# Half of the down columns of an FP4 feed-forward as products of bare values, and a first gated block in another order

## What is computed

```python
def _dequant_fp4(packed_i32, scales_f16, group_size):      # group_size 128
    shifts = jnp.arange(8, dtype=jnp.uint32) * 4
    nib = w[:, :, None] >> shifts & jnp.uint32(15)
    vals = _FP4_LUT[nib.astype(jnp.int32)].reshape(out_f, in_p * 8)
    s_full = jnp.repeat(scales_f16.astype(jnp.float32).T, group_size, axis=1)
    return vals * s_full
gate_up = jnp.einsum('bsh,oh->bso', x, w_gu)
gate, up = (gate_up[..., :I], gate_up[..., I:])            # I = 1408
h = jax.nn.silu(gate) * up
y = jnp.einsum('bsi,hi->bsh', h, w_down)                   # [512, 1408]
return y / jnp.sqrt(jnp.mean(y * y, axis=-1, keepdims=True) + EPS)
```

## Time and profile before

| | us |
|---|---|
| three runs | 937.88, 939.9, 940.07 (median 939.9) |
| profiled execution | 938.71 |
| its span | 936.7, mean granted TensorE clock 0.991 |
| stage 1 | 0 to 223 |
| first feed-forward | 225 to 527 |
| gated part | 527 to 738 |
| routed feed-forward and tail | 738 to 937 |

### The profile page before, as it was taken

One profiled execution on the slowest core, in us unless ns is written; L12 is line 12 of the kernel. 1 busy time (PEld: TensorE's weight loads), 2 busy tenths in 40 slices (PEclk: granted clock), 3 DMA queues, 4 the chain that ended last, 5 costly groups with the idle time before them and its releaser, 6 DMA issues.

```text
span 936.7 us, 13839 instructions
## 1 busy us (share of the span) xinstructions
PE 905.9 (97%) x4976; PEld 720.6 (77%) x4976; DVE 649.7 (69%) x1252; ACT 398.8 (43%) x680; POOL 299.3 (32%) x270
## 2 busy tenths in 40 slices
PE   9999999998999999999999988999999999999994
PEld 7777877886788888888777766786867878888883
DVE  6756753578987798798679676757689886644413
ACT  6443122222443634644573656455554364322221
POOL 1000100002877434434333322131226332734343
PEclk9999999999999999999999998999999999999997
DMA  8633101203210000000010200010201444142311
GB/s 284 182 94 120 47 23 46 79 14 84 52 34 1 1 1 0 1 1 1 7 38 1 101 1 1 1 45 1 90 1 24 158 157 124 51 131 75 128 68 45
DMA packets 43973, 54.20 MB, mean 58 GB/s; under 512 B 6113, under 2 KB 25858, under 8 KB 43906
## 3 DMA queue, kind: packets, MB, share of 16 engines
q1 hardware_dynamic: 42082, 49.11, 16.4%
q0 software_dynamic: 1824, 4.22, 1.4%
HBM read 42.78 MB, written 10.52 MB: 57 GB/s over the span
## 4 chain that ended last, share of the span: by engine, by line
PE 63%; DVE 6%; issue 3%; ACT 2%; POOL 1%; DVEq 0%; ACTq 0%; POOLq 0%
PE ps L41 14%; PE ps L43 14%; PE ps L42 14%; PE ps L2309 8%; PE ps L2310 8%; DVE acc L1697 2%; PE ps L2341 1%; PE ps L2415 1%; PE ps L2401 1%; PE ps L2427 1%; PE ps L2408 0%; DVE junk L1894 0%; DVE state L1795 0%; PE ps L2552 0%; PE ps L2498 0%
## 5 line engine op out<-in xcount | busy, mean ns | idle before, releaser
L1697 DVE SCALAR_TENSOR_TENSOR acc<-ps,gu_scale,acc 128x512 f32<-128x512 f32 x264 | 197.3, 748 | 47.7 <-ACT acc L1370 28.0
L2309 PE MATMUL ps<-xt_hi,gu_val 128*128 128x512 f32 x352 | 140.6, 399 | 3.6 <-PEq L71 1.9
L2310 PE MATMUL ps<-xt_lo,gu_val 128*128 128x512 f32 x352 | 137.3, 390 | 0.0
L1370 ACT ACTIVATE acc<-ps,gu_scale 128x512 f32<-128x512 f32 x88 | 60.7, 689 | 94.2 <-PE ps L2310 94.1
L2213 POOL TENSOR_TENSOR fsg<-fsg,acc 128x512 f32<-128x512 f32 x44 | 59.3, 1348 | 108.5 <-DVE acc L1697 104.4
L2309 PEld LDWEIGHTS ps<-xt_hi,gu_val 128*128 128x128 f32 x352 | 66.0, 188 | 28.6 <-DVE acc L1697 10.9
L666 POOL TENSOR_TENSOR a_rstd<-a_var,minus_half 128x1 f32<-128x1 f32 x14 | 9.0, 644 | 208.2 <-DVE a_var L553 208.2
L2310 PEld LDWEIGHTS ps<-xt_lo,gu_val 128*128 128x128 f32 x352 | 66.1, 188 | 12.1
L2218 POOL TENSOR_TENSOR fh_lo<-fsg,fh_hi 128x512 fp32r<-128x512 f32 x44 | 57.7, 1311 | 42.7 <-ACT fh_hi L1382 42.7
L41 PE MATMUL ps<-dn_hi,fh_hi 128*128 128x512 f32 x176 | 69.3, 394 | 0.0
L42 PE MATMUL ps<-dn_hi,fh_lo 128*128 128x512 f32 x176 | 68.7, 390 | 0.0
(11 more groups left out here) (297 smaller groups left out, 2166.7 us busy)
## 6 DMA issues: line engine op xcount, KB each, us to landing
mw_raw<-in_w SPq DMA_DIRECT2D x16, 512.0 KB, 3.6
a_nib<-in_gate_up_packed SPq DMA_DIRECT2D x88, 64.0 KB, 2.4
x<-x SPq DMA_DIRECT2D x16, 256.0 KB, 2.9
mw_raw<-x SPq DMA_DIRECT2D x8, 512.0 KB, 4.3
out<-mw_raw SPq DMA_DIRECT2D x8, 512.0 KB, 3.0
xt_raw<-in_xT SPq DMA_DIRECT2D x3, 1024.0 KB, 5.3
x<-in_x SPq DMA_DIRECT2D x3, 1024.0 KB, 5.9
...
```

Source lines behind the costliest of these rows:

```text
L1370: act.activation(acc[part][u // 2 % 2][:, :], ps[:, FG, :], ACT.Copy, scale=gu_scale[:, part * IT + j, 0:1]).then_inc(s_g0, 1)
L1697: dve.scalar_tensor_tensor(out=a[:, :], in0=ps[:, FG + c, :], scalar=gu_scale[:, part * IT + j, c:c + 1], in1=a[:, :], op0=ALU.mult, op1=A ...
L2309: pe.matmul(ps[:, FG + c, :], gu_val[:, o, c, :], xt_hi[b % 2][:, c, :], start=True, stop=False)
L2310: pe.matmul(ps[:, FG + c, :], gu_val[:, o, c, :], xt_lo[b % 2][:, c, :], start=False, stop=True).then_inc(s_gu, 1)
```

## The change

1. **Down columns 256 to 511** (CB = 256, two chunks of 128, NA = 2) become `down_bare(k)`: four matmuls of 512 columns with the unscaled FP4 values as weights and the high and low part of h as moving data. They give the transposed sum of one unit, [column, token], in banks FY + 2 and FY + 3. ScalarE takes both out with the column's scale (`take_bare`), GpSimd adds them up in SBUF (`add_bare`). After a block, eight transposes bring the sums back to rows (`transpose_bare`: unit 3 of the next block, unit 4 for the last, and in the gated block for the last), and ScalarE copies them (`take_chunk`).
2. **Down columns 0 to 255** stay as three products, now of 256 columns, two token tiles in a bank; at each block's start a matmul with zeros clears each of the two banks. `take` becomes `take_pair`. The scale rows are half as long.
3. **Order in the stage**: the first four `down_weights` stand ahead of the first `product`; ScalarE copies bare values in units 0 to 3 of block 0; ROWS 4 to 5, in the last block 6 to 7; the squares move behind the transposes; FRONT_SUMS 4 to 5.
4. **First gated block**: `project_qk(1)` stands whole in tile 3, `transpose_qk(1)` and half of `gate_x(0, 3)` ahead of the last `transpose_o`; sigmoid, softmax and exponentials of block 1 go forward; the last block's residual, variance and norm move into n = 1; `fold_norm_w`, the split of Wog and the squares are placed anew.
5. **Stage 1**: chunk 17's unpacking moves behind the first query tile, its values by one step; one more small DMA loads the column scales.
6. **Tail**: the roots of the selected rows are ScalarE's Sqrt and VectorE's reciprocal, not GpSimd's power.

The diff, cut to its core:

```diff
@@ take and squares of rows
-    def take(self, act, b, t, y, s_dn):
+    def take_pair(self, act, b, i, bank, s_dn):
+        act.activation(self.y[:, 2 * i:2 * i + 2, 0:CB], bank.rearrange("p (t n) -> p t n", t=2), ACT.Copy).then_inc(self.s_ye, 1)
+    def take_chunk(self, act, b, m, bank, s_yat):
+        act.wait_ge(s_yat, NA * b + m + 1)
+        act.activation(self.y[:, :, CB + m * P:CB + (m + 1) * P], bank.rearrange("p (t n) -> p t n", t=TB), ACT.Copy).then_inc(self.s_ye, 1)
@@ ScalarE
+            def bare_values(j):
+                act.activation(dn_bare[:, j, :], dn_val[:, j, CB:C], ACT.Copy).then_inc(s_da, 1)
+            def take_bare(k, m):
+                u = NA * k + m
+                act.wait_ge(s_dna, u + 1)
+                if u >= YP:
+                    act.wait_ge(s_yd, added(k - YP // NA, m))
+                act.activation(y_part[u % YP][:, :], ps[:, FY + 2 + m, :], ACT.Copy, scale=carried.dn_column[:, m, k % IT:k % IT + 1]).then_inc(s_ya, 1)
...
+                    if bare_transposes_at(b, j):
+                        for m in range(NA):
+                            rows.take_chunk(act, b - 1, m, ps[:, bare_bank(b - 1, m), :], s_yat)
                     first_group(b, j, 1)
...
                     gate_silu(b, j)
+                    if k >= 2:
+                        for m in range(NA):
+                            take_bare(k - 2, m)
@@ GpSimd
+            def add_bare(k, m):
+                u = NA * k + m
+                pool.wait_ge(s_ya, u + 1)
...
+                pool.tensor_tensor(y_acc[m][:, :], others[:, :], y_part[u % YP][:, :], ALU.add).then_inc(s_yd, 1)
+            for j in range(4):
+                down_weights(j)
...
+                    product(k)
+                    if 2 <= k < IT * NBLK - 1:
+                        add_bare(k - 2, 0)
+                    f_low(k)
+                    if k >= 2:
+                        add_bare(k - 2, 1)
@@ TensorE
+            def down_bare(k):
+                for m in range(NA):
+                    if k:
+                        pe.wait_ge(s_ya, NA * (k - 1) + m + 1)
+                    weights = dn_bare[:, j, m * P:(m + 1) * P]
+                    pe.matmul(ps[:, FY + 2 + m, :], weights, f_hi[k % HS][:, :], start=True, stop=False)
+                    pe.matmul(ps[:, FY + 2 + m, :], weights, f_lo[k % HS][:, :], start=False, stop=True).then_inc(s_dna, 1)
...
+                    if j == 0 and t % 2 == 0:
+                        pe.matmul(ps[:, FY + bank, :], zeros[:, :], gu_val[0:1, 0, :, :].rearrange("p k o -> p (k o)"), start=True, stop=False)
+                    ins = three_products(pe, ps[:, FY + bank, CB * (t % 2):CB * (t % 2 + 1)], f_hi[k % HS][:, t * P:(t + 1) * P],
+                                         f_lo[k % HS][:, t * P:(t + 1) * P], dn_hi[:, j, :], dn_lo[:, j, :], False, j == IT - 1 and t % 2 == 1)
...
+                        down_bare(k - 2)
+                        down_tiles(k - 2, range(1))
@@ tail, ScalarE and VectorE
+                act.activation(m_root[:, t:t + 1], m_var[:, t:t + 1], ACT.Sqrt).then_inc(m_rt, 1)
+                dve.reciprocal(m_rstd[:, t:t + 1], m_root[:, t:t + 1]).then_inc(m_rs, 1)
```

353 lines of the change are left out of this document (221 added, 132 removed).

## The result

The changed kernel takes 955.33 us (median of 4, 954.04 to 956.89) against 939.07 us before (937.88 to 940.07): the ratio is 1.0174, 95% interval 1.0152 to 1.0197. The forecast was 936.0 with a range to 946. It is slower by 16 us, and the range does not hold it.

The account below looks back on a forecast made before the run. TensorE, busy 97% of the span, was taken as the bound, with VectorE as full in residual units. Terms -1.9 + 3.6 - 1.8 + 2.3 + 0.4 - 5.0 - 0.7 = -3.1 gave 936.0 us, range 927 to 946.

Parts of the forecast that it names:

- I add 0.3 us a residual unit: Feed-forward units with a residual: busier GpSimd collides more often, so VectorE's period goes from 6.38 to about 6.7 us.
- less 0.8 that buffered banks absorb: Blocks 1 and 2: four residual units at 6.7 instead of 6.35 us cost +1.4, buffering takes off 0.8, leaving +0.6.
- The unit: Plain feed-forward unit: 20 matmuls at 0.227 and 12 of 256 columns at 0.120 us make 5.98 us, 0.37 less.
- Rival D: 256-column products run at the recorded length of their weight load, 0.188 us: about +24, 960 us; chance 0.05.
- Stage 1: Unpacking moved behind the query tile: TensorE's 1.97 us wait for that tile goes, -1.9 us (ends 0 and -2.0).
- Start of the stage: First feed-forward stage: eight weight products ahead delay GpSimd's first product to 235.2 us, +3.6 us (ends 2.1 and 4.4).
- rival B: Clock falls after TensorE stands 3.6 us at the feed-forward's start (+2.8), gated block's fall stays (+2.5): 941.3 us; chance 0.20.
- Blocks 1 and 2: Feed-forward blocks: plain units gain 1.87 us, but clearing banks, transposes, squares and residual units outweigh it: +1.15 us each.
- Block 3 and the stage's end: Last feed-forward block: units -2.6, transposes and clearing +1.3, squares +1.4, residual units +0.6, decay sums -0.5, adds +0.2: +0.4 us.
- First gated block and tail: Earlier key and query chain removes waits and a clock fall, -5.0 us; selected rows' roots leave GpSimd, -0.7.
- C: GpSimd nearly back to back, so VectorE's two-input residual loses two turns each time: +11, 947 us; chance 0.10.

## Why the prediction was wrong

The step that failed most is the price of GpSimd's additions: "I add 0.3 us a residual unit", "less 0.8 that buffered banks absorb", and 0.2 us for the adds in block 3. With the additions cut down 14.4 us came back. The two other failed steps are the stop in stage 1 (4.5 us off) and the landings of the scales at the start of the feed-forward stage (3.2 us off).

**The unit.** Right. Products of 256 columns in the changed kernel (timeline of TensorE, block 1):

```profile
357.55 0.28 PE L43 MATMUL ps<-dn_hi,fh_hi 128*128 128x256 f32 x1
357.66 0.28 PE L44 MATMUL ps<-dn_hi,fh_lo 128*128 128x256 f32 x1
357.78 0.28 PE L45 MATMUL ps<-dn_lo,fh_hi 128*128 128x256 f32 x1
```

They start 0.12 us apart, and a plain unit takes 6.01 us where 5.98 was worked out. Rival D is out.

**Stage 1** (-1.9, measured +2.6). The failed step is "the wait goes; the unpacking then lies in VectorE's spare time", with 0 as its worst end. What stood behind was not another tile but a store, whose landing does not move with TensorE. Rows of the kernel before show it (VectorE's 1.46 us at 76.09), and the forecast has no term for it. The removed stop is added to the stop before that store, and the longer one cost clock. The store also took 6.0 us here against 4.8 to 5.0 in the kernel before and in two variants of the changed one; why isn't shown.

**Start of the stage** (+3.6, measured +6.8). The mechanism was right: GpSimd's product 0 is late, ScalarE's high part waits for it, its group scaling stands behind, VectorE and TensorE follow. Timeline of the changed kernel:

```profile
231.40 0.67 POOL L2292 TENSOR_TENSOR dn_hi<-dn_val,scale_hi 128x256 fp32r<-128x256 f16 x1 [3.22 <-DMA scale_lo<-down_scale_parts]
...
233.34 0.68 POOL L2292 TENSOR_TENSOR dn_hi<-dn_val,scale_hi 128x256 fp32r<-128x256 f16 x1 [0.63 <-DMA scale_lo<-down_scale_parts]
...
236.20 0.67 POOL L2292 TENSOR_TENSOR dn_hi<-dn_val,scale_hi 128x256 fp32r<-128x256 f16 x1 [1.55 <-DMA scale_lo<-down_scale_parts]
...
238.70 1.26 POOL L2298 TENSOR_TENSOR fsg<-fsg,acc 128x512 f32<-128x512 f32 x1
...
239.99 0.63 ACT L1427 ACTIVATE fh_hi<-fsg 128x512 fp32r<-128x512 f32 x1 [5.72 <-POOL fsg L2298]
...
241.25 0.80 PE L2424 MATMUL ps<-xt_hi,gu_val 128*128 128x512 f32 x1 [4.03 <-ACT acc L1415]
```

Two sizes were off. The forecast timed the last pair of scales only; but the weights also wait for the first three pairs (3.22 us at 231.40, 1.55 at 236.20), so that all of the last four half-size products (0.62 us each) stand behind the third landing: product 0 comes 11.0 us after the stage's start, against 6.5 before, 4.5 later. And behind TensorE's stop of 4.4 us the clock was at half (0.50 in 241 to 247 us); 13 matmuls 0.43 instead of 0.227 us apart are some 2.6 us. That was rival B's price, given 0.20.

**Blocks 1 and 2** (+1.15 each, measured +3.5 and +4.7). The failed term is the residual units: "I add 0.3 us", "less 0.8 that buffered banks absorb". They take 6.87 us, VectorE's period grew by 0.49, and nothing is absorbed: VectorE's 6.38 us were already TensorE's 6.35. Also, it is not four units but six or seven in a block: normalisations, and unit 0 of the next block, stay at 6.7 to 6.9. The reason put down for the 0.3, that collisions become more frequent, was not it either: the residual met GpSimd's low part in every unit before too. The addition ahead of the low part moved the low part against VectorE's work, so that each residual starts 0.2 us into it instead of in its middle. The share of the transposes and squares was near: units 2 to 4 take 7.3, 7.07 and 6.65, 1.5 us more than before together, where 0.45, 0.87 and 1.4 had been added and 1.1 taken off. The run with scalings and additions both cut down shows that most of this is paid without them too (units 2 and 3 keep their 7.3 and 7.07 us).

**Block 3 and the stage's end** (+0.4, measured +7.0 and a stop of 2.9). The additions cost 5.1 of the 7. In unit 5 a chain goes round, here in the changed kernel:

```profile
493.64 1.30 POOL L2317 TENSOR_TENSOR y_acc<-y_part,y_part 128x512 f32<-128x512 f32 x1 [1.98 <-PE ps L2470]
...
497.55 0.69 ACT L1406 ACTIVATE y_part<-ps,dn_column 128x512 f32<-128x512 f32 x1 [1.41 <-POOL y_acc L2317]
...
499.50 0.67 ACT L1415 ACTIVATE acc<-ps,gu_scale 128x512 f32<-128x512 f32 x1
...
501.17 0.46 PE L2514 MATMUL ps<-soft,within 128*128 128x128 f32 x2 [1.48 <-DVE acc L1763]
```

GpSimd's first addition of the block waits for the transposes of the last block's sums (1.98 us), with the low part behind it in its queue; ScalarE's second scaling waits for that addition's buffer (1.41 us), with squares and then the group scaling behind it (499.50); VectorE waits for the group, and TensorE 1.48 us for VectorE, before sums that the change had moved here to find their inputs ready. The forecast named these queues and gave 0.2 us to them.

**First gated block and tail** (-5.7, measured -2.1 and -2.7). Right in mechanism; its own size, without the bare sums, is -8.2 by trace. The waits and the clock that the forecast added up came to 7.4. What it gave back for the adds (1.5) was too little, since the stop of 2.9 us at the stage's end came out of the same cause.

**The rivals.** C, given 0.10, had the right mechanism, the lock, though at other operations: the residuals wait for one GpSimd operation, not two, but a split or a normalisation that met a full GpSimd queue waited 3 to 4 us, in the profiles of three of the kernels tried and not in that of the changed kernel itself. What decided its low chance was "GpSimd waits for ScalarE between its operations, so gaps are to be expected". Before, GpSimd had two gaps in a residual unit, of some 3.1 and 0.74 us; in the changed kernel one of 1.36 is left, a wait for VectorE, with four operations in a row behind it, and none in units 6 and 7 of block 0, where weights and additions come together.

The Trainium skill, SBUF — State Buffer, section "SBUF: two separate sides", has the port as an exclusive lock: of a VectorE and a GpSimd operation that both need it, the one that starts first holds it for its whole length. For waits of one operation the traces agree with that rule (2.53 us for a low part beside a split, 1.62 for a residual). If the waiting operation always came next, the split of 0.68 us in unit 1 of block 1 would have waited for one addition and taken 2.0 us at most. It took 4.30, so in this case a waiting VectorE operation is at times passed over. The earlier trace rows had shown that already, and the forecast called it agreement with the rule.

What stays open: why units 2 and 3 of blocks 1 and 2 keep 7.3 and 7.07 us when scalings and additions are both cut, since clearing the banks (0.23 and 0.44 us) and the transposes (0.9) explain only 1.6 of the 2.4 us above two plain units (0.15 to 0.45 of it unit 2 paid before the change too). Open is also what decides who gets the port next: in the timeline of block 1 above the residual comes ahead of the addition at 357.73, which takes 1.75 us instead of 1.29, and the two pairs of equal meetings of L1746 (0.95 and 4.04 us, 1.37 and 5.10) ended differently. Such catches cost 3 to 4 us each and come and go from kernel to kernel, so that the division of the 16 us between the place of the weights, the additions and stage 1 is good to a few us only.
